# Banks chosen by an estimated release time, the token mask by groups of eight experts with the place of a tie summed in PSUM, and slots found by threes of experts

## The reference

```python
h = tok_ref(x, emb_2, emb_3, emb_4, proj_w, proj_b)          # (8, 1024, 128)
h = h + attn_ref(layernorm(h), ...)                           # cross, dot and cosine attention, gated
h = h + ffn_ref(layernorm(h), W_router, b_router, W_up, b_up, W_down, b_down)

def ffn_ref(x, ...):                                          # bs = 8192, E = 32, k = 256
    xf = x.reshape(bs, H)
    Sm = softmax(xf @ W_router + b_router, axis=-1)
    G_ek, idx_ek = top_k(Sm.T, k)                             # each expert's 256 tokens
    tokens = xf[idx_ek]
    up = einsum('gjkh,ghf->gjkf', tokens by groups of 4 experts, W_up) + b_up
    Eout = einsum('ekf,efh->ekh', silu(up), W_down) + b_down
    y = zeros((bs, H)).at[idx_ek.reshape(-1)].add((G_ek[..., None] * Eout).reshape(-1, H))
    return y.reshape(B, S, H)
```

## Time and profile before

| | |
|---|---|
| median of 3 runs | 1395.65 us (1395.1 to 1399.89) |
| profiled execution | 1398.12 us, its span 1395.9 us |
| PE busy | 1111.2 us (80%) |
| DVE busy | 841.5 us (60%) |
| POOL busy | 799.9 us (57%) |
| ACT busy | 673.8 us (48%) |
| mean granted TensorE clock | 0.912 |

### The profile page before, as it was taken

How to read it: one execution, slowest core, us unless ns; L and a number is a source line. 1 busy time by engine, 2 the same in 40 slices (tenths; PEclk the granted TensorE clock), 3 DMA queues, 4 the chain that set the end, 5 groups by cost and what they waited for, 6 DMA issues and landing times. The chain is left out here.

```text
span 1395.9 us, 22815 instructions
## 1 busy us (share of the span) xinstructions
PE 1111.2 (80%) x7389; PEld 970.8 (70%) x7390; DVE 841.5 (60%) x2493; ACT 673.8 (48%) x1690; POOL 799.9 (57%) x1257
## 2 busy tenths in 40 slices
PE   4569999999999999999999999999953235666572
PEld 3459788888978878888887888788852124555462
DVE  4235677777676867767776777776756875111110
ACT  0335666656565655665565566555534515212110
POOL 5355676667467657747755864545550002788875
PEclk9979999999999999999999999999985556888877
DMA  2010000000001101001010100000001000444442
GB/s 93 16 29 20 16 26 29 22 26 27 9 24 29 30 13 39 24 9 30 23 30 22 31 22 9 17 11 9 18 17 51 0 0 19 78 80 82 82 75 28
DMA packets 49080, 42.45 MB, mean 30 GB/s; under 512 B 6728, under 2 KB 44488, under 8 KB 48840
## 3 DMA queue, kind: packets, MB, share of 16 engines
q0 software_dynamic: 18432, 22.04, 8.0%
q1 hardware_dynamic: 30536, 19.00, 4.5%
HBM read 27.38 MB, written 13.63 MB: 29 GB/s over the span
## 5 line engine op out<-in xcount | busy, mean ns | idle before, releaser
L595 PE MATMUL mixed<-v,pT 128*128 128x132 f32 x2560 | 324.5, 279 | 5.2 <-issue 4.8
L595 PEld LDWEIGHTS mixed<-v,pT 128*128 128x128 f32 x2560 | 307.3, 193 | 5.6 <-issue 5.6
L1046 POOL DMA_INDIRECT gram<-in_emb,ids x192 | 191.3, 997 | 75.0 <-issue 51.7
L827 DVE TENSOR_REDUCE neg_max<-scores 128x1 f32<-128x1024 f32 (+1 forms) x192 | 199.1, 1037 | 51.9 <-PE scores L408 50.0
L975 ACT ACTIVATE probs<-scores,neg_max 128x1024 f32<-128x1024 f32 (+1 forms) x192 | 186.5, 971 | 59.9 <-DVE neg_max L827 59.8
L984 ACT ACTIVATE pT<-turned 128x512 f32<-128x512 f32 x214 | 127.4, 595 | 65.4 <-PE turned L576 62.0
L576 PE MATMUL turned<-con,probs 128*128 128x128 f32 x856 | 128.0, 277 | 30.3 <-ACT probs L975 12.1
L1088 POOL TENSOR_TENSOR zb<-row,gate 128x384 f32<-128x384 f32 x64 | 54.6, 853 | 157.5 <-DVE gate L865 156.6
L406 PE MATMUL scores<-k_hi,q_hi 128*128 128x512 f32 x320 | 136.0, 425 | 1.9 <-DVE q_lo L730 1.9
L1650 POOL DMA_INDIRECT xg<-token_table,slots x64 | 63.8, 997 | 121.1 <-DVE slots L1533 101.9
L576 PEld LDWEIGHTS turned<-con,probs 128*128 128x128 f32 x856 | 99.3, 142 | 47.5 <-ACT probs L975 19.8
(11 more groups left out here) (335 smaller groups left out, 2422.1 us busy)
## 6 DMA issues: line engine op xcount, KB each, us to landing
wd<-in_w_down SPq DMA_DIRECT2D x32, 171.0 KB
token_table<-w SPq DMA_DIRECT2D x16, 320.0 KB
out_h<-h SPq DMA_DIRECT2D x16, 256.0 KB, 2.3
gram<-in_emb,ids POOLq DMA_INDIRECT x192
wu<-in_w_up SPq DMA_DIRECT2D x8, 170.5 KB
w<-in_weights SPq DMA_DIRECT2D x1, 1174.0 KB, 6.6
xg<-token_table,slots POOLq DMA_INDIRECT x64
out_h<-yw,slots POOLq DMA_INDIRECT x64
```

The source lines that it names most:

```text
L595: last = pe.matmul(mixed[:, 0:VW], pT[:, n % 2, j * P:(j + 1) * P], vals, start=(j == 0), stop=(last_half and j == half * 4 + 3))
L827: dve.tensor_reduce(neg_max[:, n % 4:n % 4 + 1], scores[:, (n % 2) * S:(n % 2) * S + width], AX_X, ALU.max, negate=True).then_inc(maxed, 1)
L1046: pool.indirect_dma_start(gram[:, t % 4, g, :], None, emb[g], bass.IndirectOffsetOnAxis(ap=ids[:, s, t, g:g + 1], axis=0)).then_inc(gather ...
```

## The change

1. The ring's turn-taking is replaced: each use takes the bank that a small model says is free first, with a unit of 4.9 us, an item holding its bank for 2.7 us and a turned half for 1.7 us. The order of PE's instructions stays. 302 of 621 uses get another predecessor in BEFORE.
2. The mask is made in four groups of eight experts. The place of a tie is summed in one PSUM bank by four matmuls (minus a large number where `over`, the ties up to this token in the tile, all chosen over the threshold, the ties of earlier tiles), and one DVE instruction compares it with 256 and multiplies with `over + tie`. Column sums over a tile's tokens are matmuls with one column. The scan, `tie_rank`, `tie_in`, `n_over`, `room` are gone.
3. Ranks, `before`, `reached`, rows and slots are made by threes of experts. The first two threes come ahead of the experts' matmuls, the nine others stand inside the loop over experts (iteration e makes three e+2). For this `up` has one place, `down` one bank, and AHEAD is 4.
4. `thr_row` is gone: PE transposes `cand` itself. ACT's `warm` Silu, and with it the load of its table, stands ahead of the constants.

```diff
+UNIT_LONG = 4.9
+USED_AT = dict(first=1.5, half0=2.2, half1=2.6, second=4.8)
+HELD = dict(item=2.7, half=1.7)
...
-    for _user in (*PLACED.get((_s, 0), ()), *_turns, *PLACED.get((_s, 1), ())):
+    _users = [(k, "first") for k in PLACED.get((_s, 0), ())] + [(_turn, f"half{_turn[1]}") for _turn in _turns]
+    for _user, _where in _users + [(k, "second") for k in PLACED.get((_s, 1), ())]:
+        _ring = min(range(3), key=lambda j: _free[j])
+        _start = max(_s * UNIT_LONG + USED_AT[_where], _free[_ring])
+        _free[_ring] = _start + HELD["item" if isinstance(_user, int) else "half"]
...
-        _ring = (_ring + 1) % 3
...
-    AHEAD = 3
+    AHEAD = 4
...
+        def sums(g):
+            if g >= 1:
+                pe.wait_ge(sums_a, g)
+            pe.wait_ge(over_ok, g + 1)
+            for j in range(GE):
+                pe.matmul(down_bank[0:TT, j:j + 1], over[:, :, g * GE + j], ones_bf[:, 0:1], start=True, stop=True)
+            if g >= 2:
+                pe.wait_ge(chosen_ok, g - 1)
+            pe.matmul(place_bank(g), far_down[:], over[:, :, g * GE:(g + 1) * GE], start=True, stop=False)
+            pe.wait_ge(tie_ok, g + 1)
+            for j in range(GE):
+                last = pe.matmul(down_bank[0:TT, GE + j:GE + j + 1], tie[:, :, g * GE + j], ones_bf[:, 0:1],
+                                 start=True, stop=True)
+            last.then_inc(sums_t, 1)
+            pe.matmul(place_bank(g), upto_bf[:], tie[:, :, g * GE:(g + 1) * GE], start=False, stop=False)
+
+        def places(g):
+            pe.wait_ge(sums_a, g + 1)
+            pe.matmul(place_bank(g), ones_bf[0:TT, :], tile_sums[:, g, 0, :].unsqueeze(1).to_broadcast([TT, TT, GE]),
+                      start=False, stop=False)
+            pe.wait_ge(ties_ok, g + 1)
+            pe.matmul(place_bank(g), ones_bf[0:TT, :], ties_before[:, g, :, :], start=False, stop=True).then_inc(place_t, 1)
...
-            if e >= 2:
-                pe.wait_ge(hid_a, e - 1)
+            if e >= 1:
+                pe.wait_ge(hid_a, e)
...
-            if e >= 2:
-                pe.wait_ge(y_v, e - 1)
+            if e >= 1:
+                pe.wait_ge(y_v, e)
...
+        sums(0)
+        places(0)
+        rank(0)
+        rows_before(0)
+        rows(0)
+        rank(1)
+        sums(1)
+        rows_before(1)
+        rows(1)
+        places(1)
+        sums(2)
         pe.wait_ge(ones_set, 2)
         turn(0)
+        places(2)
+        sums(3)
+        places(3)
+        pe.wait_ge(chosen_ok, GROUPS)
         up(0)
         turn(1)
         for e in range(NE):
+            g = e + FIRST_TRIPLES
+            if g < len(TRIPLES):
+                rank(g)
             if e + 1 < NE:
                 up(e + 1)
+            if g < len(TRIPLES):
+                rows_before(g)
             down(e)
+            if g < len(TRIPLES):
+                rows(g)
             if e + 2 < NE:
                 turn(e + 2)
...
+        def choose(g):
...
+            dve.scalar_tensor_tensor(out=chosen[:, 1:TT + 1, at], in0=place_bank(g).rearrange("p (t e) -> p t e", e=GE),
+                                     scalar=float(TOPK), in1=reach_bf[:, :, at], op0=ALU.is_le, op1=ALU.mult
+                                     ).then_inc(chosen_ok, 1)
...
         copy_x(0)
+        choose(2)
+        count_before(3)
+        choose(3)
         copy_x(1)
         for e in range(NE):
+            g = e + FIRST_TRIPLES
+            if g < len(TRIPLES):
+                reach(g)
             weigh(e)
+            if g < len(TRIPLES):
+                find_rows(g)
             if e + 2 < NE:
                 copy_x(e + 2)
```

More of the change, by code:

```diff
@@ L1359, in _ @@
-        for q in range(4):
-            last = pe.matmul(turned[:, 0:512], ones_bf[:], over[:, q * 16:(q + 1) * 16, :], start=(q == 0), stop=(q == 3))
-        last.then_inc(sums_t, 1)
-        pe.wait_ge(masks, 2)
-        pe.wait_ge(prob_copied, 4)
-        for q in range(4):
-            last = pe.matmul(scores[:, q * 512:(q + 1) * 512], ones_bf[:], tie[:, q * 16:(q + 1) * 16, :],
-                             start=True, stop=True)
-        last.then_inc(sums_t, 1)
-        pe.wait_ge(pick_v, 1)
@@ new lines, in rows_before, with rows @@
+        def rows_before(g):
+            e0, e1 = TRIPLES[g][0], TRIPLES[g][-1] + 1
+            pe.wait_ge(rank_a, g + 1)
+            pe.matmul(rank_bank[0:TT, 3 * P:3 * P + e1 - e0], below_bf[0:TT, 0:TT], ranks[:, e0:e1, P - 1],
+                      start=True, stop=True).then_inc(before_t, 1)
+        def rows(g):
+            pe.wait_ge(reached_ok, TRIPLES[g][-1] + 1)
+            for half in range(HALVES):
+                if g >= 1:
+                    pe.wait_ge((row_v, row_a)[half], g)
+                for i, e in enumerate(TRIPLES[g]):
+                    last = pe.matmul(row_bank(half)[:, i * RW:(i + 1) * RW], reached[:, e, half * P:(half + 1) * P],
+                                     ranks[:, e, :], start=True, stop=True)
+                last.then_inc(row_t, 1)
@@ L1478, in _ @@
         dve.wait_ge(cand_ok, BITS + 1)
-        dve.wait_ge(made_g, 1)
-        dve.tensor_scalar(thr_row[:], thr_row[:], cand[0:NE, :].bitcast(F32), None, ALU.add).then_inc(thr_v, 1)
         dve.wait_ge(thr_t, 1)
         dve.tensor_copy(thr[:], turned[:, 512:512 + NE]).then_inc(thr_v, 1)
-        dve.wait_ge(thr_v, 2)
-        everywhere = thr[:].unsqueeze(1).to_broadcast([P, CT, NE])
-        for mask, op in ((over, ALU.is_gt), (tie, ALU.is_equal)):
-            for c in range(CHUNKS):
-                last = dve.tensor_tensor(mask[:, c * CT:(c + 1) * CT, :], prob[:, c:TT:CHUNKS, :], everywhere, op)
-            last.then_inc(masks, 1)
@@ L1520, in reach @@
+        find_over(0)
+        find_ties(0)
+        find_over(1)
+        count_before(0)
+        choose(0)
+        find_ties(1)
+        def reach(g):
+            e0, e1 = TRIPLES[g][0], TRIPLES[g][-1] + 1
+            dve.wait_ge(before_t, g + 1)
+            dve.tensor_copy(before[:, e0:e1], rank_bank[0:TT, 3 * P:3 * P + e1 - e0]).then_inc(before_v, 1)
+            dve.wait_ge(before_v, g + 1)
+            for e in TRIPLES[g]:
                 dve.tensor_scalar(reached[:, e, :], slot_bf[0:TT, :], before[:, e:e + 1], None,
@@ L1586, in _ @@
                            accum_out=count_a[:]).then_inc(counted_a, 1)
+        act.wait_ge(bup_in, 16)
+        act.activation(warm[:], bup[:, 0:1], ACT.Silu)
         act.wait_ge(far_in, 16)
@@ L1592, in _ @@
         act.activation(slot_bf[:], K("slot"), ACT.Identity).then_inc(made, 1)
+        act.activation(far_down[:], ident, ACT.Identity, scale=-OUT_OF_REACH).then_inc(made, 1)
+        act.activation(earlier[:], K("below")[0:TT, 0:TT].unsqueeze(2).to_broadcast([TT, TT, GE]), ACT.Identity
+                       ).then_inc(made, 1)
         act.wait_ge(made_g, 1)
-        for q in range(8):
-            act.wait_ge(rank_t, q + 1)
-            act.activation(ranks[:, 4 * q:4 * q + 4, 0:P], slot_bank(q)[0:TT, :].rearrange("p (e t) -> p e t", t=P),
-                           ACT.Identity).then_inc(rank_a, 1)
```

249 lines of the change are left out of this document (128 added, 121 removed).

## The result

The changed kernel takes 1355.71 us in the median of 4 executions (1352.44 to 1356.6); the kernel before takes 1396.6 us in 4 (1395.1 to 1399.89). The ratio is 0.9700, with a 95% interval of 0.9675 to 0.9725. The profiled execution took 1356.6 us, its span is 1354.8 us, 41.1 us less than before.

What follows compares the result with a forecast made beforehand. Bound by PE in the attention part, then an uncovered chain, then POOL: -6 - 31 - 1 + 1.5 = -36.5 us from 1398.12 gives 1361.6 profiled, 1359 median. Main spread 1351 to 1367, upper end 1373.

Steps and rivals of the forecast that it cites:

- Step 1: Attention part: PE's waits for banks emptied by DVE's k_lo shrink, up to 9.9 us; 6 us taken.
- rival C: Attention part: the banks bring nothing, the waits move on to probs; 1365 us, chance 0.12.
- Step 2: From T (thresholds known) to the first addition: new masks and threes shorten the chain to 33 us, 31 us saved.
- rival F: Chain after the thresholds: DVE's short runs of 8 elements cost twice the price, +7 us, 1366 us; chance 0.04.
- Step 3: POOL's additions: AHEAD = 4 puts one more gather into idle time, 1 us less; its rate otherwise holds.
- Step 4: Loop over experts: PE at the full clock except in the first iteration, 1.5 us lost.
- B: Loop: stays at the half clock for its nine iterations, +16 us instead of +1.5, 1373 us; chance 0.14.
- D: Loop: DVE's `reached` instructions stop POOL's DMA instructions for their length, 5 us, 1364 us; chance 0.07.
- E: Loop: ACT reloads its table between Sign and Silu, two 1.28 us loads per iteration, +40 us, 1397 us; chance 0.03.

Runs made afterwards that it cites:

- e1: The kernel before with only the changed assignment of banks; ratio 0.9901 to the kernel before.
- e2: The changed kernel with banks assigned by turns as before; ratio 0.9808 to the kernel before.
- e4: The changed kernel with gathers 1 to 3 held until all four mask groups are chosen; ratio 0.9723 to the kernel before.
- e10: The changed kernel with gathers 0 and 1 at once, 2 and 3 held until all four mask groups are chosen; ratio 0.9723 to the kernel before.
- e3: The changed kernel with three experts gathered ahead instead of four; ratio 0.9700 to the kernel before.
- e6: The changed kernel with all four mask groups ahead of the first three, same instructions; ratio 0.9764 to the kernel before.
- e11: The changed kernel with the first expert's up and down ahead of up(1), gathers 2 and 3 held until the last column sums; ratio 0.9737 to the kernel before.
- e7: The changed kernel with six more DVE instructions like `reached` in each of iterations 12 to 31; ratio 0.9744 to the kernel before.
- e8: The changed kernel with a one-column Exp ahead of ACT's comparisons in nine iterations, forcing table loads; ratio 0.9768 to the kernel before.
- e5: The changed kernel with the first expert's up product moved ahead of the last mask, its down ahead of up(1); ratio 0.9709 to the kernel before.
- e9: The changed kernel run again unchanged, on another chip's set of runs; ratio 0.9732 to the kernel before.
- e12: The changed kernel with gathers 1 to 3 held, plus 16 plain transfers of a gather's shape issued by SyncE; one execution, 1357.13 us.

## Why the prediction came out right, point by point

The time came out right, within 4 us of the likeliest, and in part by luck. Had the chain kept its 33 us beside the banks' real gain, the median would have been 5 us less, near 1350.6, just under the lower end of the range, 1351.

**The bound, right.** PE in the attention part, then a chain in the open, then POOL. From the first to the last addition POOL takes 198.7 us in the changed kernel, 198.3 before.

**Step 1, banks: -6 predicted, some -14 in e1 and e2, -15.3 in the pair of traces.** The mechanism was right in the main: what went are the waits for banks that DVE's k_lo had to empty. The size failed in the sentence "so up to 6.6 + 3.3 = 9.9 us go", and in the discount from it. First, a waits view holds only what the trace counts as idle. In numbers, for the same 5401 instructions of the middle stretch the changed kernel needs 11.2 us less: PE's idle time there falls from 44.8 us to 37.5 x 5401 / 5478 = 37.0, 7.8 us, and the busy time of the same instructions from 755.2 to 762.5 x 5401 / 5478 = 751.8, another 3.4 us. The ends of matmuls are modelled, so a short wait for a bank can lie inside a time that counts as busy; that the 3.4 us are such waits isn't shown. e1 against e2 gives the same picture, 9.3 us idle and 3.0 busy. Over the whole attention part, for the same 6503 matmuls, PE's idle time falls from 118.9 to 110.8 us and its busy time from 936.7 to 929.6. The Trainium skill (Perfetto Trace Analysis, Tensor Engine Instruction (MATMUL, LD_WEIGHTS)) says the same, that the end of a matmul is computed from its size and the semaphore comes later. In this case's traces ACT starts 0.03 to 0.11 us behind that computed end where no signal is late. Second, the two lines of the earlier trace rows aren't all: the same view has four more with k_lo (1.1, 0.7, 0.2 and 0.2 us), 12.1 us in all, and all six are gone. Third, some of it came back as new bank waits, those for pT: 6.7 us (2.2, 1.1 and the 3.4 above) where they were 2.6. So new bank waits of 4.1 us came, where the prediction allowed 2. Waits for probs did not grow: they are 9.5 + 6.4 us where they were 12.1 + 6.4. Of rival C, with the gain lost to probs, nothing came.

**Step 2, T to the first addition: 33 predicted, 38.1 and 37.2 measured; -26 instead of -31.** Up to the first slots the prices held roughly: threshold to `over` 0.7 (0.6), `choose` done at T + 6.4 (5.7), slots at T + 11.75 (10.9). Most of the 0.85 stands in the first group's mask, with comparisons of 0.69 instead of 0.62 us and column sums of 1.0 instead of 0.9 among it. From `up(0)` to the first addition it took 9.3 us (9.5). All the rest of the miss lies between: `up(0)` at T + 28.8 instead of T + 23.5. The sentence that failed is "POOL's ten gathers in this time (...) run from 1134 to 1147 and are hidden". POOL's time is hidden, but beside the gathers two of PE's signals on the path came late, 3.8 us together; held (e4), split (e10), fewer (e3) or not yet begun (e6), the delay is gone or is elsewhere. With it gone `up(0)` starts at T + 25.9 (e4, e10), so it costs 2.8 us of the path. The other 2.4 us are sizes: 0.85 up to the first slots, and some 1.6 in the second three and the masks that are left, 14.2 us from the slots to `up(0)` in e10, where the prediction had 12.6. The bound for short DVE runs at a higher price (rival F) was not needed: 8-element runs cost 0.69 us.

The trace of the kernel before already had the delay, as a piece of its chain for which no releaser is found: "1170.14 2.03 another core or an unknown queue". The lines around it show DVE waiting for nothing but its own signal, that `slot_f` is written, and going on 2.06 us later, 1.69 us behind the end of POOL's last gather there:

```profile
1169.56 0.94 POOL L1650 DMA_INDIRECT xg<-token_table,slots  x1 [0.30 <-issue]
...
1169.96 0.17 DVE L1531 TENSOR_SCALAR slot_f<-tile_no 128x18 f32<-128x18 f32 x1 [0.36 <-issue]
...
1172.19 0.18 DVE L1533 TENSOR_TENSOR slots<-slot_f,n_less 128x18 int32<-128x18 f32 x1 [2.06 <-remote]
```

ACT and PE go on at the same moment, 1172.16 and 1172.18. Read ahead of the prediction, this row could have put a price on the gathers.

**Step 3, POOL and AHEAD: right by the traces, wrong as a gain.** The changed kernel has four steps near 5.4 us at its end, before had three. But e3 shows that the fourth gather ahead costs in the chain what it saves at the end.

**Step 4, the loop: right in size, not in place.** POOL's first nine steps take 60.1 us, 59.0 before, so 1.1 us are lost, where 1.5 were put on the half clock of the first iteration. That iteration loses nothing: POOL's first step is 6.42 us. `up` and `down` run at the full clock from the second iteration on, and POOL waits for `yw` once more after the first addition, by 0.3 us. The steps over 6.4 us are waits for an earlier addition to land.

**The rivals.** B didn't happen, but its mechanism is real: e11 brought it about, with `up` at 2.91 us and steps of 10.5 and 7.4, by giving PE a pause in front of the loop. What spoke against it in the prediction, that the half clock follows a pause of PE, is what e11's rows show. D is refuted by e7. E is refuted twice: the loop has no table load, and eighteen of them, forced in e8, cost 2 to 4 us and not 20, since rival E put them on the cycle without asking what ACT waits for there. At its price of 2 to 4 us E could not have made the kernel slower.

## What to carry to other kernels

A wait for a buffer can cost more than the waits view of PE lists, as here; to bound it from above, compare how many instructions PE does in a long window at the full clock, or try the buffers alone. Work that is hidden on its own engine can still go with late signals of others: here, beside POOL's gathers, those of PE and DVE, so gathers belong where no signal is awaited. A piece of the chain that has no releaser is worth a look before the work beside it is called hidden. Bringing one expert forward is worth nothing when the following ones can't follow, and a pause of PE that it opens can cost the clock.

## What was not expected of the hardware

Semaphore signals of PE came late beside POOL's indirect gathers, 0.45 to 3.03 us at the same two places in all six executions with ten gathers there (the changed kernel, e2, e5, e7, e8, e9), by 3.4 to 3.9 us in sum (1.81 + 1.96, 1.79 + 1.96, 0.45 + 3.03, 1.83 + 1.97, 1.16 + 2.71, 0.45 + 2.95). They came 0.04 us late beside plain transfers with twice the traffic (e12).

The end of the second delay is steadier than its length. The first is over in the midst of the gathers (0.9 us behind the end of the sixth in the changed kernel, e2, e3 and e7). For the second, the instruction that is let go starts 1.3 to 1.9 us behind the end of the last of POOL's gathers in a row, and so does that at the places with one delay: 1.69 us in the kernel before, 1.70 (e1), 1.68 (changed), 1.71 (e2), 1.58 (e5), 1.69 (e7), 1.77 (e8), 1.50 (e9), and for the signals that moved 1.71 (e4), 1.33 (e10), 1.31 (e11), 1.71 (e12) and 1.89 (e6). In e4 a gather's tokens are there, and let PE go on, 1.65 us behind the end of its instruction (1136.16 to 1137.81), so the release falls about where the last gather has landed. Not every signal is held: others pass beside the same gathers on time, as ACT's to PE in the changed kernel (end 1128.63, start 1128.68). Which are held, and by what, stays open.

It is not PE alone: in the kernel before and in e1 DVE's own signal to itself is late by 2.06 and 2.70 us. DVE's ends are not of the modelled kind, so there it is the signal, or its receipt, that is late; whether PE's matmul is late too isn't settled, since its end in the trace is modelled. The Trainium skill (SBUF — State Buffer, Who interferes with whom) says of the ports into SBUF that "PE and ACT never wait on anyone"; what is late here is a signal, and no run shows a wait for a port.

A forced switch of ACT's tables took 1.3 us and nothing more: the Silu before the load ends at 1150.57 in e8, the load starts at 1150.59 and the next activation at 1151.88.
